# Leaving the rows of three LayerNorms uncentred and centring the weights that read them

## What is computed

```
x = layernorm(x + L0(x, adj))    # attention, softmax over the row
x = layernorm(x + L1(x, adj))    # attention, softmax over the column, then ELU
x = layernorm(x + L2(x, adj))    # attention, softmax over the row, weights with bias, then ELU
x = layernorm(x + L3(x, adj))    # sum over neighbours, one 128x128 weight, bias
layernorm(x) = (x - mean(x)) / sqrt(var(x) + 1e-5)     # over the 128 features
```

## Time and profile before

| | |
|---|---|
| runs of the kernel | 443.39, 443.77 (median), 444.32 us |
| span of the profiled execution, first to last instruction | 440.8 us |
| own time of the profiled execution | not shown; the median stands 2.97 us above its span |
| PE busy | 366.6 us (83%) |
| PEld busy | 326.6 us (74%) |
| DVE busy | 368.5 us (84%) |
| ACT busy | 316.0 us (72%) |
| POOL busy | 294.1 us (67%) |
| mean granted clock of TensorE | 0.952 of 2.4 GHz |

### The profile page before, as it was taken

One profiled execution on the slowest core, in us unless ns is written; L12 is line 12 of the kernel. 1 busy time (PEld: TensorE's weight loads), 2 busy tenths in 40 slices (PEclk: granted clock), 3 DMA queues, 4 the chain that ended last, 5 costly groups with the idle time before them and its releaser, 6 DMA issues. The chain is left out here.

```text
span 440.8 us, 9222 instructions
## 1 busy us (share of the span) xinstructions
PE 366.6 (83%) x2770; PEld 326.6 (74%) x2777; DVE 368.5 (84%) x1406; ACT 316.0 (72%) x814; POOL 294.1 (67%) x430
## 2 busy tenths in 40 slices
PE   2689999999977776976787799899999789898860
PEld 1689999999877776876787799889888674454540
DVE  0067999999999999999999988889898987887862
ACT  2378999999855865655755867778787667877853
POOL 3226889977656644545463676888788867788782
PEclk9999999999988989898898999999999999999995
DMA  6999664000000000000000000000000000012122
GB/s 159 220 248 250 142 127 78 0 2 1 3 1 2 0 1 1 1 1 2 1 1 1 1 1 2 0 2 2 0 1 4 0 1 1 25 72 74 67 77 75
DMA packets 8756, 18.19 MB, mean 41 GB/s; under 512 B 1280, under 2 KB 2560, under 8 KB 8704
## 3 DMA queue, kind: packets, MB, share of 16 engines
q0 software_dynamic: 2304, 8.39, 10.0%
q1 hardware_dynamic: 5280, 8.72, 5.6%
q10 hardware_dynamic: 1120, 0.46, 0.5%
HBM read 21.76 MB, written 4.19 MB: 59 GB/s over the span
## 5 line engine op out<-in xcount | busy, mean ns | idle before, releaser
L486 PE MATMUL o_ps<-h_scaled,PT 128*128 128x129 f32 (+1 forms) x1536 | 190.3, 285 | 2.5 <-DVE PT L911 1.2
L486 PEld LDWEIGHTS o_ps<-h_scaled,PT 128*128 128x128 f32 x1536 | 186.2, 202 | 3.5 <-issue 1.7
L690 ACT ACTIVATE X<-y,offset,rstd 128x128 f32<-128x128 f32 x256 | 105.0, 481 | 47.9 <-POOL offset L277 47.9
L911 DVE SCALAR_TENSOR_TENSOR PT<-rows_ps,factors,MT 128x512 f32<-128x512 f32 x128 | 88.8, 737 | 0.6 <-PE rows_ps L473 0.2
L434 PE MATMUL h_ps<-wx,xT 128*128 128x130 f32 x384 | 58.8, 301 | 24.8 <-DVE smax L866 24.1
L434 PEld LDWEIGHTS h_ps<-wx,xT 128*128 128x128 f32 x384 | 52.5, 208 | 31.7 <-issue 31.5
L268 POOL TENSOR_TENSOR rstd<-var_eps,neg_half 128x4 f32<-128x4 f32 x64 | 68.9, 1077 | 5.0
L983 DVE BATCH_NORM_STATS2 stats<-y 128x6 f32<-128x128 f32 x256 | 56.0, 281 | 6.7 <-DVE y L963 0.5
L283 POOL TENSOR_TENSOR elu_exp<-elu_exp,X 128x512 f32<-128x512 f32 x32 | 40.8, 1274 | 15.0 <-ACT elu_exp L684 14.7
L258 POOL TENSOR_TENSOR h_scaled<-hx,factors 128x516 f32<-128x516 f32 x32 | 33.7, 1052 | 19.9 <-ACT factors L650 10.2
L906 DVE SCALAR_TENSOR_TENSOR PT<-MT,empty_col,edge 128x512 f32<-128x512 bf16 x64 | 44.3, 744 | 0.0
(11 more groups left out here) (104 smaller groups left out, 596.0 us busy)
## 6 DMA issues: line engine op xcount, KB each, us to landing
MT<-adj_by_j POOLq DMA_DIRECT2D x16, 512.0 KB, 8.8
X<-x SPq DMA_DIRECT2D x16, 256.0 KB, 6.5
out<-X SPq DMA_DIRECT2D x16, 256.0 KB, 2.0
w_rel<-w SPq DMA_DIRECT2D x1, 256.0 KB, 5.1
w_back<-w_by_output ACTq DMA_DIRECT2D x1, 192.0 KB, 3.3
wx<-w_by_input ACTq DMA_DIRECT2D x1, 192.0 KB, 5.5
bias<-b ACTq DMA_DIRECT2D x1, 64.0 KB, 4.6
bias<-b SPq DMA_DIRECT2D x1, 64.0 KB, 5.8
```

The costliest lines, as they stand in the source:

```text
L486: last = pe.matmul(o_ps[it.b][:, ic, first:1 + D], PT[:, it.b, jc, ic * P:(ic + 1) * P], h_scaled[:, it.b, jc, first:1 + D], start=(jc == ...
L690: last = act.activation(X[:, g, c, :], y[:, b, c, :], ACT.Identity, bias=offset[:, b, c:c + 1], scale=rstd[:, b, c:c + 1])
L911: dve.scalar_tensor_tensor(out=PT[:, it.b, c, :], in0=rows_ps[:], scalar=factors[:, it.b, 1, c:c + 1], in1=m, op0=ALU.max, op1=ALU.mult, * ...
```

## The change

POOL makes a matrix `centre` = identity - 1/128. PE multiplies the projections of layers 1 and 2 (with their score columns, 260 columns together) by it in slot -3 into `rows_ps`, and layer 3's weight in slot 46 into `h_ps`; ACT copies the products back over the weights in slots -2 and 47. PE waits for these copies before the first `rows_ps` of item 0 and before the first product of layer 3. For the items of layers 0 to 2, POOL no longer computes `neg_mean` and `offset`, and ACT writes y x rstd by a Copy with a scale from a tile and waits for `rstd` alone. Layer 3's items keep the whole normalization. The branch for other `adj` values is as before.

```diff
--- before.py
+++ after.py
@@ -26,6 +26,7 @@
 
 LAST_ATTENTION, ATTENTION_END = G * LAYERS - 4, G * LAYERS + 3
 FLAG_SLOT = G * LAYERS + 6
+CENTRE_SLOT, CENTRE_LATE_SLOT = -3, G * LAYERS - 2
 R_EIGHTY, EXPONENT, BIAS, Z, RZ, ABOVE, BELOW, HINGE, WEIGHT = range(9)
 LOWEST, BIG = -430.0, 3e38
 
@@ -100,6 +101,7 @@
         split = sb("split", [P, 4, 3, C, D], BF16)
         rest = sb("rest", [P, 2, C, D])
         ident = sb("ident", [P, P])
+        centre = sb("centre", [P, P])
         ones_bf = sb("ones_bf", [P, 1], BF16)
         col_sum = sb("col_sum", [P, 2, C])
         flag_own = sb("flag_own", [P, 2])
@@ -212,6 +214,8 @@
             pool.wait_ge(sem("ident_zero"), 1)
             pool.affine_select(out=ident[:], in_=ident[:], compare_op=ALU.not_equal, fill=1.0, base=0,
                                pattern=[[-1, P]], channel_multiplier=1).then_inc(sem("ident"), 1)
+            pool.wait_ge(sem("ident"), 1)
+            pool.tensor_scalar(centre[:], ident[:], -1.0 / P, None, ALU.add).then_inc(sem("centre"), 1)
             pool.memset(neg_half[:], -0.5)
             pool.memset(eps_tile[:], EPS)
             pool.memset(minus_one[:], -1.0).then_inc(sem("pool_const"), 1)
@@ -273,7 +277,7 @@
                 pool.tensor_tensor(neg_mean[:, it.b, :], mean_var[:, it.b, :, 0], minus_one[:], ALU.mult)\
                     .then_inc(sem("neg_mean"), 1)
                 pool.wait_ge(sem("rstd"), it.done)
-                pool.wait_ge(sem("neg_mean"), it.done)
+                pool.wait_ge(sem("neg_mean"), it.of_layer)
                 pool.tensor_tensor(offset[:, it.b, :], neg_mean[:, it.b, :], rstd[:, it.b, :], ALU.mult)\
                     .then_inc(sem("offset"), 1)
 
@@ -315,7 +319,6 @@
                     elu_low(at(-1))
                 if at(-2):
                     find_rstd(at(-2))
-                    find_offset(at(-2))
                 if at(1) and at(1).l == 1:
                     scale_h(at(1))
                 if n == G + 8:
@@ -463,6 +466,8 @@
                 else:
                     pe.wait_ge(sem("factors"), halves(it))
 
+                if it.done == 1:
+                    pe.wait_ge(sem("centred"), 1)
                 last = item(it.done - 2)
                 if last and last.l == 1:
                     pe.wait_ge(sem("edge_lin"), last.of_layer * C)
@@ -503,6 +508,14 @@
                               start=True, stop=True).then_inc(sem("b2_ps"), 1)
                 if at(0):
                     attend(at(0))
+                if n == CENTRE_SLOT:
+                    pe.wait_ge(sem("centre"), 1)
+                    pe.matmul(rows_ps[:, 0:260], centre[:], wx[:, 1:3, :].rearrange("p l w -> p (l w)"),
+                              start=True, stop=True).then_inc(sem("centred_ps"), 1)
+                if n == CENTRE_LATE_SLOT:
+                    pe.wait_ge(sem("hx"), G * LAYERS)
+                    pe.matmul(h_ps[:, 1, 0:D], centre[:], w_rel[:, 0, :], start=True, stop=True)\
+                        .then_inc(sem("centred_ps"), 1)
 
             def gather(it):
 
@@ -522,6 +535,8 @@
             def project_sum(it):
 
                 pe.wait_ge(sem("sum_taken"), it.of_layer)
+                if it.g == 0:
+                    pe.wait_ge(sem("centred"), 2)
 
                 if it.g < 2:
                     pe.wait_ge(sem("y_lin"), G - 1 + it.g)
@@ -684,15 +699,30 @@
                 act.activation(elu_exp[:, :, :], elu_low_arg[:, :, :], ACT.Exp, scale=-1.0)\
                     .then_inc(sem("elu_exp"), 1)
 
-            def normalize(b, g, offset_sem, done, name):
-                act.wait_ge(offset_sem, done)
+            def take_scaled(it):
+
+                act.wait_ge(sem("rstd"), it.done)
                 for c in range(C):
-                    last = act.activation(X[:, g, c, :], y[:, b, c, :], ACT.Identity, bias=offset[:, b, c:c + 1],
-                                          scale=rstd[:, b, c:c + 1])
-                last.then_inc(sem(name), 1)
+                    last = act.activation(X[:, it.g, c, :], y[:, it.b, c, :], ACT.Copy, scale=rstd[:, it.b, c:c + 1])
+                last.then_inc(sem("x_new"), 1)
 
             def take_norm(it):
-                normalize(it.b, it.g, sem("offset"), it.done, "x_new")
+                act.wait_ge(sem("offset"), it.of_layer)
+                for c in range(C):
+                    last = act.activation(X[:, it.g, c, :], y[:, it.b, c, :], ACT.Identity,
+                                          bias=offset[:, it.b, c:c + 1], scale=rstd[:, it.b, c:c + 1])
+                last.then_inc(sem("x_new"), 1)
+
+            def take_centred(n):
+
+                if n == CENTRE_SLOT + 1:
+                    act.wait_ge(sem("centred_ps"), 1)
+                    act.copy(wx[:, 1:3, :].rearrange("p l w -> p (l w)"), rows_ps[:, 0:260])\
+                        .then_inc(sem("centred"), 1)
+                if n == CENTRE_LATE_SLOT + 1:
+                    act.wait_ge(sem("centred_ps"), 2)
+                    act.copy(w_rel[:, 0, :], h_ps[:, 1, 0:D])\
+                        .then_inc(sem("centred"), 1)
 
             def flag(it):
 
@@ -723,9 +753,10 @@
                 if near_column_layer:
                     take_next(at)
                 if at(-3) and at(-3).l != 1:
-                    take_norm(at(-3))
+                    take_scaled(at(-3))
                 if at(-2) and at(-2).l == 1:
-                    take_norm(at(-2))
+                    take_scaled(at(-2))
+                take_centred(n)
                 if not near_column_layer:
                     take_next(at)
                 if at(2) and at(2).l == 1:
```

## The result

| | before | after |
|---|---|---|
| runs of the kernel, median (lowest to highest) | 443.58 us (442.67 to 444.32) | 436.76 us (436.32 to 437.06) |
| ratio of the two, 95% interval | | 0.9845 (0.9809 to 0.9880) |
| span of the profiled execution | 440.8 us | 435.0 us |
| ScalarE, GpSimd busy | 316.0, 294.1 us | 301.4, 273.1 us |

The kernel became 6.8 us faster. The forecast was 440.3 us and the range ended at 438.4 us: the direction was right, the size was not. About 1 us of the miss lies in the base. The changed kernel's profiled execution took 436.8 us for a span of 435.0, so 1.8 us lie around a span (1.8 to 2.0 in the other executions with a trace); by that the profiled execution of before took about 442.6 us, an estimate, and not the median, and the forecast from it should have begun there.

The account below looks back on a forecast made before the run. TensorE bounds layer 0, VectorE layer 1, a round of latencies layer 2, a ScalarE-VectorE-GpSimd round layer 3. Gains 0.3 + 0.62 + 0.39 + 0.84 + 1.34 = 3.5 us, from 443.77 to 440.3 us; range 438.4 to 442.2 us.

Parts of the forecast that it names:

- the base: Whole run: the median lies 2.97 us above the profiled span, taken as unchanged time around it; 443.77 us to subtract from.
- the centring product at the start: Slot -3, TensorE: two passes of 260 columns, about 1.0 us, hidden in 1.44 us idle for `xT`; no cost counted.
- rival (b): Start: the added product brings the clock up sooner, second projection 0.94 us shorter; 439.3 us in all, chance 0.15.
- Layer 0, 0.3 us: Late layer 0: ScalarE-led slots return to TensorE's pace, three waits each up to 0.13 us shorter; 0.3 us (0 to 0.4).
- The sentence on collisions: VectorE and GpSimd sharing a port: any new meeting is paid in full, and none would come from the removal alone.
- Layer 1, 0.62 us: Layer 1: X no longer waits for `offset`, so two 0.31 us waits for ScalarE's hinge go; 0.62 us (0.3 to 0.62).
- Crossing, 0.39 us: Passage into layer 2: earlier, shorter X copies cut VectorE's wait from 0.74 to 0.35 us; gain 0.39 us (0 to 0.8).
- Layer 2, 0.84 us: Layer 2: shorter copies save 0.12 us a slot in seven slots, limited by VectorE's `smax_own`; 0.84 us (0 to 1.0).
- End, 1.34 us: End of layer 2: shorter, earlier last copies bring VectorE's `split` cast sooner; 1.34 us (0.7 to 1.6), kept through layer 3.
- (a): Copies into X: they do not get shorter, staying at 481 ns; 1.7 us gained, 442.1 us in all, chance 0.17.
- (c): Layers 0 and 2 and the end: everything covered, only two hinge waits go; 0.62 us gained, 443.2 us, chance 0.07.
- (d): Layer 2: GpSimd's earlier `h_scaled` collides with VectorE's `y` in 14 slots, costing 5.5 us; 445.8 us, chance 0.03.

## Why the prediction was wrong, point by point

- **The step that failed: the centring product at the start costed at nothing.** That its products "stand behind the first projection, in the 1.44 us that TensorE idles for `xT`" is true of its 1.07 us. But that the product changes the clock for what stands behind it was only rival (b), with 0.15 and 0.94 us. What the runs showed in its place: put into the kernel before or taken out of the changed one, the product moves the time by 1.1 to 2.2 us between medians, and it is worth 1.4 us between the two profiles, more than the 0.94 us of (b), because the transposes ahead of the second projection (1.11 and 0.42 us, now 0.83 and 0.27) and the small product behind it (0.58, now 0.39) were at the lower level too. Why the clock rises when it does stays open: one trace shows it rise as early without the product. (In the profiled executions 0.77 us of it went again on weights that landed later; their landing lies between 7.1 and 8.0 us over the executions of both sides.)
- **The base.** "The median lies 2.97 us above its span, which I take as what lies around it": what lies around it is 1.8 to 2.0 us. The profiled execution was one of the quicker runs, and the sum was taken from the median instead of from it: about 1.2 us too high.
- **Layer 0, 0.3 us:** right for the ScalarE-led slots. The 0.37 us at the entry into layer 1 were missing. The sentence on collisions, that "none would come out of the removal alone", missed the other way round: taking work out of GpSimd's queue shifts what stands behind it against VectorE, and can end a collision as well as begin one.
- **Layer 1, 0.62 us:** 0.73 measured; both waits went. The reason given, the earlier release, is enough but was not needed: the shorter copies alone do it as well.
- **Crossing, 0.39 us:** 1.58 us. The wait of 0.74 fell to 0.35 as said, but that was one of two such slots: (2,5) and (2,6) both went from 6.93 to 6.54 us. The rest, 0.77 us, is the slot from (2,1) to (2,2), in which TensorE stood at the half clock; where it does not, the round of `offset`, the copies and `hx` takes that time from the kernel before (33.88 us). The forecast did not look at that slot.
- **Layer 2, 0.84 us:** 0.81, by the mechanism named, with VectorE's `smax_own` next in line. Undoing the length alone takes it all back.
- **End, 1.34 us:** 1.30, and kept through layer 3 (63.16 and 63.09 us).
- **Rivals:** (a) falls with 389 ns; (c) with the stages; (d) did not come, `y` and the layer-2 slots show no new stretch.

The steady gains, without start and clock, add up to 0.67 + 0.73 + 0.81 + 0.81 + 1.30 = 4.3 us against 3.5 forecast: inside what the ends of the terms allowed (4.4). The range failed because (b) was taken at 0.94 us, the base at the median, and the 0.77 us at the crossing at nothing.

Open: why the clock rises and falls where it does in a given execution, and so how the 6.8 us of the medians, 1.0 more than the 5.8 us between the two spans, divide up. The spans of the kernel before vary from 439.7 to 444.5 us over 23 runs beside one experiment, and only its two profiled executions have a trace.

## What to carry to other kernels

Work that hides in an engine's idle time is not free of effect: ask what it does to that engine's clock for the instructions behind it, above all at the start, where nothing covers them. Cut the span at instructions common to both kernels and compare stage by stage; the time of a run mixes gains of 0.1 us with microseconds of chance, while the stages keep them apart. And when instructions leave a queue, look at which neighbours on the other engine the ones behind them now meet or miss.

## What the hardware showed that was not expected

- A product whose result nobody reads made the kernel before faster, 441.64 against 443.80 us. In its trace TensorE's clock was up for the second projection, 1.13 instead of 2.07 us; in another trace of the kernel before it rose as early without the product, and fell again.
- Stretches of 3.4 us at half clock come in layer 1. In the one at 251.9 us of the kernel before TensorE was busy for 3.40 of 3.40 us; in the 3.40 us ahead of it, for 1.50. Where one falls decides 0.77 us in the changed kernel, and nothing in the one before, whose ScalarE takes the same time in its place.
- A VectorE instruction on 128x4 numbers (`col_tmp`) took 0.33 or 0.71 us according to when GpSimd's neighbour had begun, and GpSimd's `offset` 0.20 or 0.61 us.
